# Attention scores as plain float32 products of 32 rows, one per head, and probabilities turned in 128-key chunks

## What is computed

```python
q = _split_heads(queries @ W_q + b_q)          # 8 x 16 heads x 512 tokens x 32
k = _split_heads(keys @ W_k + b_k)             # 8 x 16 heads x 77 keys x 32
v = _split_heads(values @ W_v + b_v)
scores = jnp.einsum('bhqd,bhkd->bhqk', q, k) / jnp.sqrt(jnp.float32(d))
scores = jnp.where(mask == 0, jnp.float32(-1000000.0), scores)
attn = jax.nn.softmax(scores, axis=-1)
out = jnp.einsum('bhqk,bhkd->bhqd', attn, v)   # then out @ W_o + b_o
```

## Time and profile before

| | |
|---|---|
| median of 3 runs | 956.01 us (954.81 to 960.93) |
| the profiled execution | 959.13 us; its span from the first to the last instruction 957.2 us |
| mean granted clock of TensorE | 0.975 |
| PE busy | 910.8 us (95%) |
| DVE busy | 666.7 us (70%) |
| ACT busy | 376.7 us (39%) |
| POOL busy | 337.6 us (35%) |
| one step of the loop | 58.7 us |
| score products | 384, in 64 blocks of six |

### The profile page before, as it was taken

The page is one execution under the profiler, slowest core; times in us unless marked ns, Lnnn a source line. Parts: engine busy times, 40 slices in busy tenths (PEclk is TensorE's granted clock), DMA queues, the critical chain, the costliest instruction groups (busy, mean ns, idle before and its releaser), DMA issues.

```text
span 957.2 us, 14638 instructions
## 1 busy us (share of the span) xinstructions
PE 910.8 (95%) x4476; PEld 755.9 (79%) x4476; DVE 666.7 (70%) x1128; ACT 376.7 (39%) x1403; POOL 337.6 (35%) x310
## 2 busy tenths in 40 slices
PE   5898999999999999999779999999999999999997
PEld 4774888888888888888678788888888888888775
DVE  3362466665656556566668888979888798888957
ACT  3152220101011111101386656746467555666611
POOL 2000243232323232314236444344544354433733
PEclk9997999999999999999779999999999999999999
DMA  5944201221303020204513022220312214030021
GB/s 180 340 137 175 90 1 47 86 71 62 114 19 131 0 88 16 73 23 126 188 27 99 21 91 65 80 75 22 100 53 90 66 23 135 15 90 21 17 77 45
DMA packets 72347, 76.04 MB, mean 79 GB/s; under 512 B 38567, under 2 KB 40871, under 8 KB 72303
## 3 DMA queue, kind: packets, MB, share of 16 engines
q1 hardware_dynamic: 72303, 75.49, 24.5%
HBM read 52.60 MB, written 22.87 MB: 79 GB/s over the span
## 4 chain that ended last, share of the span: by engine, by line
PE 42%; DVE 4%; ACT 2%; issue 2%; POOL 2%; POOLq 0%; DVEq 0%
PE shared_ps L75 31%; PE score_ps L75 5%; PE shared_ps L1147 4%; ACT probs L1353 1%; PE shared_ps L1110 1%; PE shared_ps L1180 1%; POOL probs L1502 1%; DVE score_ps L1659 1%; DVE xT_lo L1616 0%; DVE x_and_res L1705 0%; DVE top_s L1664 0%; DVE pT_lo L1643 0%; POOL x_and_res L1517 0%; DVE w_o_lo L1826 0%; DVE y L1683 0%
## 5 line engine op out<-in xcount | busy, mean ns | idle before, releaser
L1353 ACT ACTIVATE probs<-score_ps,top_s 128x77 f32<-128x77 f32 x512 | 159.0, 359 | 37.3 <-DVE top_s L1664 37.1
L1353 ACT ACTIVATION_READ_ACCUMULATOR probs<-score_ps,top_s 128x1 f32 x512 | 122.8, 240 | 0.0
L1502 POOL TENSOR_TENSOR probs<-probs,per_total 128x616 f32<-128x616 f32 x64 | 82.7, 1309 | 66.2 <-DVE per_total L1671 66.0
L1495 POOL TENSOR_TENSOR rstd<-ve,half_power 128x1 f32<-128x1 f32 x64 | 42.3, 661 | 156.8 <-DVE ve L1694 152.3
L724 POOL TENSOR_TENSOR vals<-qs_prod 128x512 f32<-128x512 f32 x32 | 41.0, 1293 | 125.7 <-DVE qs_prod L806 125.7
L715 POOL TENSOR_TENSOR mix_rstd<-mix_ve,half_power 128x1 f32<-128x1 f32 x32 | 22.1, 689 | 170.8 <-DVE mix_ve L825 170.8
L1659 DVE COPY_PREDICATED score_ps<-hidden,masked 128x616 f32<-128x616 int32 x64 | 66.6, 1040 | 11.5 <-PE score_ps L75 11.5
L1360 ACT ACTIVATE pT_hi<-shared_ps 103x512 fp32r<-103x512 f32 (+1 forms) x96 | 54.8, 612 | 45.8 <-PE shared_ps L1147 45.3
L674 ACT ACTIVATE v_sb<-v_ps 128x512 f32<-128x512 f32 x32 | 18.9, 594 | 131.2 <-PE v_ps L75 131.2
L681 ACT ACTIVATE qT_hi<-vals 128x512 fp32r<-128x512 f32 x32 | 19.3, 628 | 119.2 <-POOL vals L724 103.6
L1643 DVE TENSOR_TENSOR pT_lo<-shared_ps,pT_hi 103x512 fp32r<-103x512 f32 (+1 forms) x96 | 64.5, 684 | 0.0
(11 more groups left out here) (218 smaller groups left out, 2656.1 us busy)
## 6 DMA issues: line engine op xcount, KB each, us to landing
x_tok<-in_x SPq DMA_DIRECT2D x8, 1024.0 KB, 6.3
x_res<-in_x SPq DMA_DIRECT2D x8, 1024.0 KB, 8.2
x_between<-mix_x SPq DMA_DIRECT2D x32, 256.0 KB, 2.0
x<-x_between SPq DMA_DIRECT2D x8, 1024.0 KB, 5.6
x_tok<-x_between SPq DMA_DIRECT2D x8, 1024.0 KB, 5.7
out<-y_out SPq DMA_DIRECT2D x32, 256.0 KB, 2.0
wqkv_sb<-in_w_qkv SPq DMA_DIRECT2D x4, 768.0 KB, 7.4
keys_split<-w_q_hi SPq DMA_DIRECT2D x8, 154.0 KB, 5.7
```

Source lines behind the costliest of these rows:

```text
L1353: nc.scalar.activation(probs[:, t % 2, j * KEYS:(j + 1) * KEYS], score_ps[:, g, k * KEYS:(k + 1) * KEYS], ACT.Exp, bias=top[:, t % 2, j:j ...
L1495: nc.gpsimd.tensor_tensor(rstd[:, n:n + 1], ve[:, n:n + 1], half_power[:], ALU.pow).then_inc(rstd_ready, 1)
L1502: nc.gpsimd.tensor_tensor(p, p, per_total[:, t % 2, h * heads:(h + 1) * heads].unsqueeze(2) .to_broadcast([P, heads, KEYS]), ALU.mult).the ...
```

## The change

**Scores.** Queries and keys stay plain float32 and are not split. The features are placed anew (`by_head`, `by_place`) so that row group b (rows 32b to 32b + 31) of chunk c holds one head. `score` takes a head's 32 rows of `q` as the stationary operand (128 tokens) and the same 32 rows of `keys` as the moving one (77 columns), into columns c x 77 of bank b. Per quarter and half h: 4 chunks x 2 row groups, alternating, eight products. The keys need no zeros, no second part, one load. All four Q are needed for the first block of a batch.

**Order.** Q3 moves ahead of F3 (the last feed-forward product), on all engines and in `BANK_ORDER`. DVE's `split_q` computes nothing now; it waits and counts the bank as freed.

**Probabilities.** Each half of the heads (616 columns) is four chunks of 128 and one of 104. Bank 0 has the four of the first half, bank 1 those of the second, bank 2 the two short ones: ten transposes per quarter. `turn_probs` waits for each half by itself. `weigh_values` takes 9 products per g as before, of 128 or 104 rows. The values are loaded in 24 pieces per batch instead of 12.

**Opening.** A key unit is product, bias and scale, one store; the keys have three slots of their own. `kv_prod` of the mixer shares memory with `q`.

```diff
+HALF = 2 * GK
+CHUNK = 128
+TAIL = HALF - 4 * CHUNK
+BANKS = [(0, 4, CHUNK), (4, 4, CHUNK), (8, 2, TAIL)]
...
+def by_head(w):
+    return w.rearrange("p (a c r) -> p c a r", a=2, c=NC)
+def by_place(w):
+    return w.rearrange("p (c a r) -> p c a r", a=2, c=NC)
+def chunk_at(h, k):
+    return 4 * h + k if k < 4 else 8 + h
+def group_chunks(g):
+    h, first = g // 2, 2 * (g % 2)
+    return [(m, chunk_at(h, first + m), TAIL if first + m == 4 else CHUNK) for m in range(3)]
...
-            bias_keys(0)
             for n in range(NKEY):
-                if n + 1 < NKEY:
-                    bias_keys(n + 1)
-                dve.wait_ge(k_hi_ready, n + 1)
...
-                nc.vector.tensor_tensor(out_lo[:, n % SLOTS, 0:half_rows], k_val[:, n % 2, :], out_hi[:, n % SLOTS, 0:half_rows].bitcast(F32),
-                                        ALU.subtract).then_inc(k_lo_ready, 1)
+                wait_reuse(dve, k_stored[n % 3], 16 * (n // 3))
+                nc.vector.tensor_scalar(k_val[:, n % 3, :], prod[n % 2][:, 0:half_rows],
+                                        bias_k[:, n // 2:n // 2 + 1], float(XHD) ** -0.5, ALU.add,
+                                        ALU.mult).then_inc(prod_used, 1)
...
 def load_keys(sp, k_dram, hand, i):
-    for part in range(2):
-        src = k_dram[part].rearrange("(g j d) r -> j d g r", j=GH, d=XHD)
-        for j in range(GH):
-            sp.dma_start(hand.k_block[part][j * XHD:(j + 1) * XHD, :, j * KEYS:(j + 1) * KEYS].bitcast(F32),
-                         src[j][:, :, bass.ds(i * KEYS, KEYS)]).then_inc(hand.k_loaded, 16)
+    sp.dma_start(hand.keys[:], k_dram.rearrange("(g p) r -> p g r", p=P)[:, :, bass.ds(i * KEYS, KEYS)]).then_inc(hand.k_loaded, 16)
...
             def score(i, s, t, h):
-                if t == 0:
-                    pe.wait_ge(k_loaded, nth(i, 1, 0) * (16 * 2 * GH))
-                    pe.wait_ge(q_hi, nth(i, NC, 2 * h + 1))
-                    pe.wait_ge(freed, s.emptied_before(f"Q{2 * h + 1}"))
+                if t == 0 and h == 0:
+                    pe.wait_ge(k_loaded, nth(i, 1, 0) * 16)
+                    pe.wait_ge(q_hi, nth(i, NC, NC - 1))
...
-                for g in (2 * h, 2 * h + 1):
-                    last = split_matmuls(nc, score_ps[:, g, 0:GK],
-                                         [([q[:, g, tok] for q in qT], [k[:, g, :] for k in k_block])])
-                last.then_inc(scored, 1)
+                for c in range(NC):
+                    for b in (2 * h, 2 * h + 1):
+                        head = slice(b * XHD, (b + 1) * XHD)
+                        last = nc.tensor.matmul(score_ps[:, b, c * KEYS:(c + 1) * KEYS], q[head, c, tok], keys[head, c, :],
+                                                start=True, stop=True)
+                        if c == NC - 1:
+                            last.then_inc(scored, 1)
 
             def turn_probs(i, s, t, c):
-                if c == 0:
-                    pe.wait_ge(normed, nth(i, NT * 2, 2 * t + 1))
+                if c < 2:
+                    pe.wait_ge(normed, nth(i, NT * 2, 2 * t + c))
...
-                for g in range(GROUPS):
-                    last = nc.tensor.transpose(shared_ps[s.bank(use)][0:size, g * P:(g + 1) * P],
-                                               probs[:, t % 2, g * GK + at:g * GK + at + size], ident[:])
+                _, chunks, size = BANKS[c]
+                for n in range(chunks):
+                    at = c * HALF + n * CHUNK if c < 2 else n * HALF + 4 * CHUNK
+                    last = nc.tensor.transpose(shared_ps[s.bank(use)][0:size, n * P:(n + 1) * P],
+                                               probs[:, t % 2, at:at + size], ident[:])
...
             def split_q(i, s, c):
-                biased_remainder(q_hi, nth(i, NC, c), qT[0][:, c, :], qT[1][:, c, :], shared_ps[s.bank(f"Q{c}")][:],
-                                 bias_q[:, c:c + 1])
+                dve.wait_ge(q_hi, nth(i, NC, c))
+                dve.wait_ge(freed, s.emptied(f"Q{c}") - 1)
+                dve.sem_inc(freed, 1)
```

More of the change, by code:

```diff
@@ L103, in prepare @@
         raw_v = wqkv_sb[:].rearrange("p c n -> p (c n)")[:, NC * D:2 * NC * D].rearrange("p (c n) -> p c n", c=NC)
-        ctxT = [sb(f"ctxT_{k}", [P, NC, rows], F32R) for k in ("hi", "lo")]
+        row = (rows + LINE - 1) // LINE * LINE
+        flat = [t[:].rearrange("p c n -> p (c n)") for t in scratch]
+        ctxT = [[f[:, c * row:c * row + rows] for c in range(NC - 1)] + [sb(f"ctxT_{k}", [P, row], F32R)[:, 0:rows]]
+                for f, k in zip(flat, ("hi", "lo"))]
         a_sb = ffn[:, 1, 0:NC * RANK].rearrange("p (c n) -> p c n", c=NC)
@@ L164, in _ @@
                 c, h = n // 2, n % 2
[L165 to L168, removed]
+                sp.wait_ge(prod_used, n + 1)
+                sp.dma_start(k_dram[c * P:(c + 1) * P, h * half_rows:(h + 1) * half_rows],
+                             k_val[:, n % 3, :]).then_inc(k_stored[n % 3], 16)
                 if n == NC + 1:
@@ L239, in _ @@
                 pe.wait_ge(prod_used, n - 1)
-                pieces = [([t[:, k, at:at + size] for t in ctxT], [w[:, k, :] for w in w_v]) for k in range(NC)]
+                pieces = [([t[k][:, at:at + size] for t in ctxT], [w[:, k, :] for w in w_v]) for k in range(NC)]
                 split_matmuls(nc, prod[n % 2][0:size, :], pieces).then_inc(prod_ready, 1)
@@ L318, in copy_turned @@
                                      ACT.Copy).then_inc(wT_ready, 1)
-            act.wait_ge(k_lo_ready, NKEY)
+            for n in range(3):
+                act.wait_ge(k_stored[n], 16 * len(range(n, NKEY, 3)))
             copy_turned(0)
@@ L1020, in turned_bank @@
         def turned_bank(s, t, c):
-            return shared_ps[s.bank(f"P{t}{c}")][0:KC[c][1], :].rearrange("p (g n) -> p g n", g=GROUPS)
+            _, chunks, size = BANKS[c]
+            return shared_ps[s.bank(f"P{t}{c}")][0:size, 0:chunks * P].rearrange("p (k n) -> p k n", k=chunks)
         @block.sync
@@ L1340, in split_q @@
                 act.wait_ge(filled, s.filled(use))
-                nc.scalar.activation(qT[0][:, c, :], shared_ps[s.bank(use)][:], ACT.Identity,
+                if c == 0:
+                    act.wait_ge(scored, 2 * nth(i - 1, NT * 2, NT * 2 - 1))
+                nc.scalar.activation(q[:, c, :], shared_ps[s.bank(use)][:], ACT.Identity,
                                      bias=bias_q[:, c:c + 1]).then_inc(q_hi, 1)
@@ L1441, in _ @@
             split_q(1, s, 2)
+            split_q(1, s, 3)
             split_probs(0, s, 3, 0)
```

170 lines of the change are left out of this document (80 added, 90 removed).

## The result

The changed kernel takes 989.48 us (median of 4 runs, 983.98 to 991.05), 1.031 times the kernel before (95% interval 1.028 to 1.034). I had forecast 970: the direction was right, but the loss is 31.5 us where I had 14 (the kernel before, run beside it, took 957.96, the median of 4). The profiled execution's span is 989.2 us, 32.0 more than before.

A forecast was written before the change was run, and what follows sets the result against it. PE (TensorE), busy 95% of the 957.2 us span, was taken to set the loop step. Terms summed to +13.7 (-7.0 + 1.4 + 11.3 + 11.6 - 3.3 - 0.8 - 1.0 + 1.5); less 1.2, 970 us, range 938 to 1018.

The forecast's parts named there:

- The rest: Remaining effects outside the main terms: DVE's saved work in the loop 0, handover -0.8, half-wise transposes -1.0, longer blocks before loop +1.5.
- handover: At the handover, DVE's last query remainder no longer holds the block's end and PE: -0.8 us.
- Q3 before F3: At each step's end, Q3 no longer covers DVE's list, so PE waits: 1.93 us for six steps, +11.6 (bounds +6, +14).
- Transposes: Ten transposes of probabilities instead of twelve per quarter, 0.109 us each on PE: -7.0 us.
- The score products: 512 plain float32 products, two passes each, replace 384 float32r ones; loads two at a time: +1.4 us (bounds -19.8, +57.5).
- paired loads: In a score block, the two row groups load at the same time; mark: starts in pairs of about 0.11 us.
- the rival of independent groups: Row groups run beside each other and the full array, loads hidden, nothing drains: -30 us, 940; chance 0.20.
- Changing the row size: Entering and leaving a block of 32-row products loses 0.2 us each on PE: +11.3 us (bounds 0, 19.3).
- terms for edges and products: Per loop step, 1.4 us for entering and leaving 32-row blocks and 0.2 for the score products.
- Opening: Keys stored once, unsplit; PE's wait for w_q_lo and part of the following half clock go: -3.3 us (bounds 0, -4.3).
- half-normed transposes: Transposes may start when half of the heads are normalised, where PE had three waits of 1.8 us: -1.0 us.
- The undisturbed step: One step of the attention loop was forecast at 60.5 to 61.5 us for 58.70.

The follow-up runs named there:

- e3_first_bank: Changed kernel with V0, the first value product, waiting only for the first bank of the last quarter's probabilities, V1 for the other two: 974.3 us, ratio 1.015.
- e8_align_bank: Changed kernel with the filler behind the keys 8 words instead of 12, and V0 waiting only for the first bank it reads: 964.8 us, ratio 1.006.
- e10_four_23: Changed kernel with 8-word filler, V0's narrowed wait, and four row groups in one visit only in quarters 2 and 3 of steps 1 to 6: 965.3 us.
- e9_chunks_only: Kernel before with only the 128-key probability chunks (ten transposes for twelve, values in 24 pieces), scores as before: 955.3 us, ratio 0.994.
- e1_align: Changed kernel with the filler behind the keys 8 words instead of 12, so later buffers begin at a multiple of 64 bytes: 987.8 us, ratio 1.032.
- e2_shift_before: Kernel before with 8 words more behind the mask, so later buffers begin 32 bytes off a multiple of 64: 966.9 us, ratio 1.009.
- e6_all: Changed kernel with 8-word filler, V0's narrowed wait and all four row groups in one visit: 976.5 us, ratio 1.020.
- e11_q3_last: Changed kernel with 8-word filler, Q3 back behind the last transposes, and V0 ahead of a step's first block: 979.4 us, ratio 1.020.

## Why the prediction was wrong, point by point

**The step that failed** is the sum itself: it holds terms only for places where the list of instructions changes, each at full clock. Two costs lay outside. **Place in memory:** the mixer stood under "The rest" at nothing but the handover; it cost 8.1 us, and 0.36 a step in the loop (60.09 in e3_first_bank, 59.73 in e8_align_bank). The allocation was there to be read in the diff. **The clock behind the stall:** I forecast a wait of 2 us in every step and charged its length only, although the profile of before showed PE idle and at half clock together, in the start (0.76, 9.3 us idle). It cost 7.6 us in steps 2 and 3 (65.8 + 64.6 - 2 x 61.4) and part of the closing's 8.1, in which V0 waits 2.4 and some 10 us run at half clock.

**Q3 before F3** was the right mechanism, named as forecast (DVE pT_lo), and mis-sized: idle time per step rose by 2.5 and I had 1.93. I let DVE's last split end at 631.3, where the earlier trace rows have its start at 631.26; with its 0.41 and the 0.24 from its end to the product the term becomes 2.6. In all it cost more than the 11.6 of the forecast: narrowing V0's wait alone, which left 0.7 of it, gave 15 back in the changed kernel and 23 in the aligned one, clock included.

**Transposes** (-7.0): alone they gave 4.4 in the time; PE did lose them, and waits took half back.

**The score products** (+1.4): right for a block by itself (eight pairs 0.90 for six products 0.85). Pairs 0.112 apart stood in the prediction as the mark of paired loads. The rival of independent groups was right in part, too: a group loads and streams by itself, beside the others, but its own pass takes 0.112, so two groups give what two paired loads give. The Trainium skill ("TensorEngine Tiling (Array Packing)", Key Properties) says that different tiles load and multiply in parallel; the rows above agree, 1.13 for four groups and 1.12 for two.

**Changing the row size** (+11.3): 0.24 a visit for both edges, I charged 0.41; nothing is lost between row groups. And I had no term for two blocks in a row, which overlap: of the four visits that neither the stall nor the wait for `xT_lo` hides, each of the two single ones costs 0.29 more than the products it replaces, and the two double ones cost 0.10 and 0.03 less. That is 0.45 a step, where my terms for edges and products had 1.6.

**Opening, handover, half-normed transposes** (-3.3, -0.8, -1.0): the first mixer product comes 2.7 earlier, without the wait for `w_q_lo`. (One execution each; in the others it starts at 90.5 and 91.5 us with the old opening, at 85.8 to 88.8 and once at 92.7 with the new.) The other two, from PE's waits after:

```profile
PE score_ps L1147 <- PEq L472: 1.3, 1, 1.3
PE shared_ps L1161 <- POOL probs L1518: 1.0, 1, 1.0
```

They were 1.99 and 1.8, so -0.7 and -0.8.

The undisturbed step came out at 61.35, in the range I gave (60.5 to 61.5), but by errors that cancel: the stall and the place were more, the edges less. That it fell in the range was luck.

## What to carry to other kernels

Before costing a change, compare where every buffer behind the changed ones begins, not only which instructions change. A forecast stall on a busy TensorE is charged with its length and with a stretch at half clock behind it as the upper end. And when a change takes work off the engine that sets the time, read first who is next in line there: here, of the 1.0 us a step that e10_four_23 took off PE, 0.8 became waits for DVE, and of e9_chunks_only's 0.97 about half.

## What the runs showed of the hardware

- With buffers 32 bytes off a multiple of 64, the mixer's float32r products of 512 columns take 0.234 us where they take 0.227, in both directions of the test (e1_align, e2_shift_before). It doesn't hold for every product: the value products of the loop, moved as well, keep 0.230. Whether 64 or a larger power of two is what counts isn't told apart: the good places here are multiples of 256 as well.
- A 32-row plain float32 pass of 77 columns takes 0.112 us in its row group, and groups run side by side: 32 passes of four groups (1.13, e6_all) in the time of sixteen of two (1.12).
- PE fell from 2.4 to 1.2 GHz during the wait at V0 (2.4 to 2.9 us) or within 2 us behind it three times of six in the changed kernel and four of six in e1_align, the closing counted; in e11_q3_last at the second of two waits of 0.9 and 1.0 us some 13 us apart, or within about 1 us behind it, in each step; and in e3_first_bank and e8_align_bank never behind the 0.72 left at V0, once behind 1.03 there, and twice behind the 0.7 at the first output projection. What decides between a wait that is followed by a fall and one that isn't stays open.
